# Quantised attention in a decoder kernel: constant waits, two heads scored together, the bias on GpSimd, four score slots

## The chip, the cores and the metric

One core of one Trainium2 chip. The metric is the device time of one execution in microseconds. The kernel is one program that holds a whole two-layer decoder; the change touches one of its stages.

## The reference, cut to what matters

Input x is 32 x 64 tokens of width 256, and ctx has the same shape. There are six sublayers; the fifth is the quantised cross-attention, with 16 heads of width 16 over all 2048 tokens at once (every query sees all 2048 keys):

```python
q = (x @ Wq + bq).reshape(1, B * N, H, hd)          # B*N = 2048, H = hd = 16
kv = (cond @ Wkv + bkv).reshape(1, -1, 2, H, hd)
q = _fq_sym(q * scale, axis=-1)                     # rounded to 127 steps per token and head
k = _fq_sym(k, axis=-1)
v = _fq_sym(v, axis=2)
attn = jax.nn.softmax(jnp.einsum('bhqd,bhkd->bhqk', q, k), axis=-1)
attn = _fq_unsigned(attn, axis=-1)                  # rounded to 255 steps of the row's maximum
out = jnp.einsum('bhqk,bhkd->bhqd', attn, v)
```

The row maximum of the softmax is always 255 steps, so exp(score - max + ln 255), rounded to an integer, is the quantised row up to its sum.

## The kernel before

The stage is `quantised_attention`. Its first block makes the quantised operands: `QT` (queries, transposed, bf16, 128 tile-and-head-pair slices; an even head's 48 rows begin at partition 0, an odd head's at 64), `KTt` (keys, likewise) and `Vi` (values as whole numbers). The second block is the loop that the change rewrites. It has 256 units: 16 tiles of 128 queries by 16 heads. A unit n is one head of one tile, 128 queries by 2048 keys. For each unit:

- TensorE (`score`) multiplies 48 rows by 512 keys four times, into two pairs of PSUM banks, a pair (1024 keys) for each half. Six of the eight banks serve as three such pairs, taken in turn (`pair_banks`). A group of two matmuls waits on `score_out` until the pair's earlier content was read, and raises `scored`.
- VectorE reads a pair with one `tensor_scalar` that also reduces: it scales by the negative query step `nsq`, writes 1024 fp32 scores to `S32` and their minimum to `mn`, and raises `score_out`. After both halves a 128x1 operation makes `ebias` = min of the two + ln 255 and raises `biased`. `S32` is the old context buffer `ctxT`, with two slots.
- ScalarE takes the exponential of the 2048 scores with that bias into `e16`, as uint16, with the sum in `esum`, and raises `exped`. There are four slots, in the buffers `xh` and `xl`.
- The sync engine issues a DMA transpose of `e16` to `PT` (four slots, in `xnT`), which lands on `laid[slot]`. It waits for `exped` and for the mix four units earlier.
- TensorE (`mix`), six units behind (`LAG`), multiplies 16 transposed blocks by `Vi` and raises `mixed`; after eight heads ScalarE copies the result out (`output`).
- GpSimd copies each pair's query slice from `QT` to one of six slots `Qs`, three pairs ahead, since a loop can't index `QT` for a weight load by a register as it is written here.

The order on each engine is written by hand. The first 48 units are written out, then a hardware loop (`Fori`) of four rounds has a body of 48 units whose waits and indices are worked out in registers, and the last 16 units and the drain are written out again. `wait_apart` is a wait followed by a separate semaphore instruction. Blocks end with all engines waiting for each other.

Of the kernel before, what the change touches and what calls it, by code (L numbers as in the profile page):

```python
# [23 lines left out]
ds = bass.ds  # L24
# [1334 lines left out]
def quantised_attention(nc, m, w):  # L1359
# [16 lines left out]
    q_here, scored, score_out, biased, exped, mixed, normed, chain2 = (m.sem(f"e_{n}") for n in (  # L1376
        "q_here", "scored", "score_out", "biased", "exped", "mixed", "normed", "chain2"))
# [4 lines left out]
    with ExitStack() as own:  # L1382
# [186 lines left out]


        class Unit:

            def __init__(self, i, u):
                self.i, self.u, self.j = i, u, u % H
                self.known = isinstance(i, int)

            def n(self, per=1, times=1):

                return self.i * (BODY // per * times) + self.u // per * times

            def back(self, d):
                return Unit(self.i, self.u - d)

            def exists(self):
                return not self.known or 0 <= self.i * BODY + self.u < N

            def at_least(self, k):

                return not self.known or self.i * BODY + self.u >= k

        def loop(eng, step, extra=0):

            for u in range(BODY):
                step(Unit(0, u))
            with eng.Fori(1, N // BODY) as i:
                for u in range(BODY):
                    step(Unit(i, u))
            for u in range(N % BODY + extra):
                step(Unit(N // BODY, u))
# [5 lines left out]
        with nc.Block() as block:  # L1605
            @block.gpsimd
            def _(pool):

                def fetch(x):

                    pair = x.n(2)
                    if x.at_least(2 * QSLOTS):
                        m.wait_apart(pool, scored, (pair - (QSLOTS - 1)) * 4)
                    pool.tensor_copy(Qs[:, x.u // 2 % QSLOTS, :],  # L1614
                                     QT[:, ds(pair, 1), :].rearrange("p a b -> p (a b)")).then_inc(q_here, 1)

                def step(x):
                    if not x.exists():
                        return
                    ahead = x.back(-2 * QAHEAD)  # L1620
                    if x.u % 2 == 0 and ahead.exists():
                        fetch(ahead)

                for p in range(QAHEAD):
                    fetch(Unit(0, 2 * p))
                loop(pool, step)

            @block.sync
            def _(sp):
                def step(x):  # L1630
                    m.wait_apart(sp, exped, x.n() + 1)
                    if x.at_least(SLOTS):
                        m.wait_apart(sp, mixed, x.n() - (SLOTS - 1))
                    sp.dma_start_transpose(PT[:, x.u % SLOTS, :, :], e16[x.u % SLOTS].bitcast(F16)).then_inc(laid[x.u % SLOTS], 16)
                loop(sp, step)

            @block.tensor
            def _(pe):
                def score(x):
                    j = x.j  # L1640
                    rows = slice(64 * (j % 2), 64 * (j % 2) + 48)
                    if j % 2 == 0:
                        m.wait_apart(pe, q_here, x.n(2) + 1)
                    for hf in range(2):
                        if x.at_least(2):
                            m.wait_apart(pe, score_out, x.n(1, 2) + hf - 2)
                        elif 2 * x.u + hf >= 3:
                            pe.wait_ge(score_out, 2 * x.u + hf - 2)
                        b = pair_banks(2 * x.u + hf)
                        for q in range(2):  # L1650
                            mm = pe.matmul(m.bank[b + q], Qs[rows, x.u // 2 % QSLOTS, :],  # L1651
                                           KTt[rows, j // 2, (2 * hf + q) * BLK:(2 * hf + q + 1) * BLK],
                                           start=True, stop=True)
                        mm.then_inc(scored, 1)

                def mix(x):
                    j = x.j
                    m.wait_apart(pe, laid[x.u % SLOTS], x.n(SLOTS, 16) + 16)
                    if j % 8 == 0 and x.at_least(16):
                        m.wait_apart(pe, normed, x.n(8) - 1)  # L1660
                    for k in range(KT):
                        mm = pe.matmul(m.bank[6 + j // 8][:, j % 8 * HD:(j % 8 + 1) * HD], PT[:, x.u % SLOTS, k, :],  # L1662
                                       Vi[:, k, j, :], start=(k == 0), stop=(k == KT - 1))
                    mm.then_inc(mixed, 1)

                def step(x):
                    if x.exists():
# [377 lines left out]
```

## Time and profile before

| | |
|---|---|
| three timed runs, median | 3037.68 us (3037.57 to 3043.3) |
| profiled execution | 3038.51 us |
| its span, first to last instruction | 3036.7 us |
| mean granted TensorE clock | 0.792 |
| TensorE matmuls busy | 2498.7 us, 82% |
| VectorE busy | 1932.5 us, 64% |
| ScalarE busy | 1482.0 us, 49% |
| GpSimd busy | 409.3 us, 13% |

Busy times are sums over the whole program, whose stages have different limits. A clock of 1.00 is 2.4 GHz and 0.50 is 1.2 GHz. PE is TensorE's matmuls, PEld its weight loads, DVE is VectorE, ACT is ScalarE, POOL is GpSimd, SPq the sync engine's queue. In brackets behind an instruction stand the idle time before it and what ended it.

### The profile page before, as it was taken

What the parts mean: (1) busy time and instruction counts of PE and PEld (TensorE: products, weight loads), DVE (VectorE), ACT (ScalarE), POOL (GpSimd) and SP (SyncE); (2) the same over time, 40 slices, a digit from 0 to 9 for tenths busy, and PEclk for the clock granted to TensorE, in tenths of its full rate; (3) what the DMA queues carried; (4) which work ended last, traced back from release to release, by engine and by line L of the source; (5) the groups of instructions that cost most, each with busy time, mean ns of one, the idle gap of its engine ahead of it and who ended that gap; (6) DMA issues with size and microseconds to landing.
All of it is one profiled execution on the core that took longest, in us unless ns stands there. A gap on an engine that the chain in (4) does not pass through costs nothing. (4 is left out here: it accounts for less than half of the span.)

```text
span 3036.7 us, 50228 instructions
## 1 busy us (share of the span) xinstructions
PE 2498.7 (82%) x16570; PEld 1358.9 (45%) x16570; DVE 1932.5 (64%) x3686; ACT 1482.0 (49%) x2055; POOL 409.3 (13%) x454
## 2 busy tenths in 40 slices
PE   6874775999979999999664888787878865999998
PEld 3333554555547777777552222222222232444444
DVE  6995556667743333333456998888888845666665
ACT  5552332444433333333232776666666633666664
POOL 0001220111012222333133000000000001001100
PEclk9886776999979999999776555555555567999999
DMA  2000000000010000000000999999999940000001
GB/s 83 0 0 19 0 0 12 16 26 21 21 29 18 18 17 17 17 17 9 21 0 18 177 176 169 165 169 162 171 163 171 173 71 17 24 23 16 23 23 36
DMA packets 594876, 175.35 MB, mean 58 GB/s; under 512 B 548642, under 2 KB 594212, under 8 KB 594724
## 3 DMA queue, kind: packets, MB, share of 16 engines
q1 hardware_dynamic: 594724, 173.44, 29.6%
q8 instruction: 81, 1.33, 0.2%
q14 instruction: 71, 0.58, 0.1%
HBM read 37.07 MB, written 2.10 MB: 13 GB/s over the span
## 5 line engine op out<-in xcount | busy, mean ns | idle before, releaser
L1682 DVE TENSOR_SCALAR_CACHE_REDUCE ctxT<-psum,e_nsq 128x1024 f32<-128x1024 f32 x512 | 637.2, 1282 | 74.2 <-issue 54.1
L1651 PE MATMUL psum<-e_KT,e_Qs 48*128 48x512 bf16 x1024 | 519.9, 611 | 181.7 <-DVE ctxT L1682 151.0
L1703 ACT ACTIVATE xh<-ctxT,e_ebias 128x2048 uint16<-128x2048 f32 x128 | 256.2, 2002 | 134.0 <-DVE e_ebias L1686 134.0
L1703 ACT ACTIVATE xl<-ctxT,e_ebias 128x2048 uint16<-128x2048 f32 x128 | 256.2, 2002 | 119.2 <-DVE e_ebias L1686 119.2
L1651 PEld LDWEIGHTS psum<-e_KT,e_Qs 48*128 48x128 bf16 x1024 | 67.3, 104 | 415.8 <-issue 408.1
L103 PE MATMUL psum<-xh,d_WT 128*128 128x512 f16 x768 | 229.4, 381 | 2.6 <-DVE d_WT L1214 2.6
L1662 PEld LDWEIGHTS psum<-e_Vi,xnT 128*128 128x128 f16 x4096 | 129.5, 105 | 216.8 <-issue 216.8
L1233 DVE TENSOR_TENSOR d_ACC<-psum,d_ACC 128x512 f32<-128x512 f32 x128 | 82.5, 686 | 171.1 <-PE psum L1287 171.1
L103 PE MATMUL psum<-xh,f_WA 128*128 128x512 f16 x544 | 152.7, 383 | 13.9 <-DVEq L1896 11.8
L103 PE MATMUL psum<-xh,c_Wx 128*128 128x512 f16 x576 | 161.3, 383 | 0.8 <-DVE X L960 0.8
L1662 PE MATMUL psum<-e_Vi,xnT 128*128 128x16 f16 x4096 | 152.5, 175 | 8.1 <-DMA xnT<-xh 4.5
L1912 DVE SCALAR_TENSOR_TENSOR X<-psum,f_route,X 128x256 f32<-128x256 f32 x272 | 112.8, 477 | 70.3 <-PE psum L1972 70.3
L1139 POOL TENSOR_TENSOR d_sq<-d_oS 128x512 f32<-128x512 f32 x64 | 99.1, 1548 | 420.8 <-ACT d_oS L1183 420.8
L1972 PE MATMUL psum<-f_W2H,f_hh 128*128 128x256 f16 x544 | 151.0, 278 | 3.1 <-DVE f_hh L1924 3.1
L1972 PE MATMUL psum<-f_W2L,f_hh 128*128 128x256 f16 (+1 forms) x544 | 150.8, 277 | 0.0
L1227 DVE SCALAR_TENSOR_TENSOR d_y<-d_gt,d_oS 128x512 f32<-128x512 f32 x64 | 44.3, 693 | 145.6 <-ACT d_oS L1183 145.6
L1614 POOL COPY e_Qs<-e_QT 128x128 bf16 (+1 forms) x128 | 37.3, 294 | 722.9 <-PE psum L1651 722.6
L1287 PE MATMUL psum<-d_WoT,d_y 128*128 128x256 f32 x512 | 122.7, 382 | 5.8 <-DVE d_y L1227 5.7
L974 DVE SCALAR_TENSOR_TENSOR X<-psum,c_route,X 128x256 f32<-128x256 f32 x288 | 119.3, 476 | 11.8 <-PE psum L103 11.0
L1875 ACT ACTIVATE f_h<-psum 128x512 f32<-128x512 f32 x68 | 40.6, 597 | 156.4 <-PE psum L103 156.4
L1902 DVE TENSOR_TENSOR f_pr<-psum,f_h 128x512 f32<-128x512 f32 x68 | 47.0, 692 | 108.9 <-ACT f_h L1875 108.9
L1167 ACT ACTIVATE d_kT<-psum 128x512 f32<-128x512 f32 x64 | 38.2, 597 | 159.3 <-PE psum L103 159.3
(312 smaller groups left out, 4965.9 us busy)
## 6 DMA issues: line engine op xcount, KB each, us to landing
d_Wn<-in_L_attn_w_qkv SPq DMA_DIRECT2D x16, 384.0 KB, 3.2
f_W<-in_L_ffn_w_routed SPq DMA_DIRECT2D x32, 176.0 KB, 2.5
ctx_rows<-in_ctx SPq DMA_DIRECT2D x1, 2048.0 KB, 8.6
X<-in_x SPq DMA_DIRECT2D x1, 2048.0 KB, 14.0
c_Wgu<-in_L_ffn_rg SPq DMA_DIRECT2D x16, 128.0 KB, 2.1
c_Wgu<-in_L_ffn_rw SPq DMA_DIRECT2D x16, 128.0 KB, 2.2
c_Wd<-in_L_ffn_rw SPq DMA_DIRECT2D x16, 128.0 KB, 2.2
d_Wn<-in_L_attn_w_gate SPq DMA_DIRECT2D x16, 128.0 KB, 3.0
```

The source lines that it names most:

```text
L103: mm = pe.matmul(out, lhsT(a, k), rhs(b, k), start=(n == 0), stop=(n == len(terms) - 1))
L974: last = dve.scalar_tensor_tensor(m.X[:, t, :], m.bank[4 + 2 * (q % 2) + j // 2][:, (j % 2) * D:(j % 2 + 1) * D], R.route[:, t, ds(e0 + sl ...
L1139: pool.tensor_tensor(sq[:, :], o, o, ALU.mult).then_inc(squared, 1)
L1233: last = dve.tensor_tensor(a2, m.bank[6 + half][:, :], a2, ALU.add)
L1287: mm = pe.matmul(m.bank[6 + j // 2][:, (j % 2) * D:(j % 2 + 1) * D], y[:, j * P:(j + 1) * P], WoT[:, slot, :], start=True, stop=True)
L1651: mm = pe.matmul(m.bank[b + q], Qs[rows, x.u // 2 % QSLOTS, :], KTt[rows, j // 2, (2 * hf + q) * BLK:(2 * hf + q + 1) * BLK], start=True, ...
L1662: mm = pe.matmul(m.bank[6 + j // 8][:, j % 8 * HD:(j % 8 + 1) * HD], PT[:, x.u % SLOTS, k, :], Vi[:, k, j, :], start=(k == 0), stop=(k == ...
L1682: dve.tensor_scalar(S32[:, sl, hf * HALF:(hf + 1) * HALF].rearrange("p (a b) -> p a b", a=2), m.psum[:, b:b + 2, :], nsq[:, ds(x.n(), 1)], ...
L1703: act.activation(e16[x.u % SLOTS], S32[:, x.u % 2, :], ACT.Exp, bias=ebias[:, x.u % 2:x.u % 2 + 1], scale=-1.0, accum_out=esum[:, ds(x.n() ...
L1902: dve.tensor_tensor(pr[:, st % 2, 0, :], m.bank[1][:, :], h1[:, st % 2, 0, :], ALU.mult).then_inc(product, 1)
L1912: last = dve.scalar_tensor_tensor(m.X[:, t, :], m.bank[4 + 2 * (q % 2) + j // 2][:, (j % 2) * D:(j % 2 + 1) * D], R.route[:, t, ds(e, 1)], ...
L1972: mm = pe.matmul(m.bank[4 + 2 * (q % 2) + j // 2][:, (j % 2) * D:(j % 2 + 1) * D], a, b, start=(n == 0), stop=(n == len(terms) - 1))
```

## The change

All of the loop is written out: `loop` calls a step for each of the 256 units with a plain number, so that waits and indices are constants, and `wait_apart` goes. TensorE reads its query weights from `QT` directly, and `Qs` with its copies and the semaphore `q_here` go. `score` is called for an even unit alone and scores it and the next one: in each half and quarter an even head's matmul (partitions 0 to 47) is followed by the odd head's (64 to 111), into two different bank pairs, four matmuls behind one wait. VectorE reads both heads' first halves, then both second halves. `ebias` is made by GpSimd, and `S32`, `mn` and `ebias` have four slots in place of two (`Smore` is new memory). The exponential, the transpose, the mix and the output keep their work.

```diff
-        BODY, SLOTS, LAG, QAHEAD, QSLOTS = 48, 4, 6, 3, 6
-        Qs = sb("Qs", [P, QSLOTS, P], BF16)
-        mn = sb("mn", [P, 2, 2])
-        ebias = sb("ebias", [P, 2])
+        SLOTS, LAG = 4, 6
+        mn = sb("mn", [P, SLOTS, 2])
+        ebias = sb("ebias", [P, SLOTS])
...
+        Smore = sb("Smore", [P, 2, TOK])
...
-        S32 = m.ctxT
+        S32 = [m.ctxT[:, 0, :], m.ctxT[:, 1, :], Smore[:, 0, :], Smore[:, 1, :]]
...
+        def loop(step, extra=0):
+
+            for n in range(N + extra):
+                step(n)
...
             @block.gpsimd
             def _(pool):
...
+                def step(n):
+                    sl = n % SLOTS
+                    pool.wait_ge(score_out, n // 2 * 4 + 3 + n % 2)
+                    if n >= SLOTS:
+                        pool.wait_ge(exped, n - SLOTS + 1)
+                    pool.tensor_scalar(ebias[:, sl:sl + 1], mn[:, sl, 0:1], mn[:, sl, 1:2], LN255,
+                                       ALU.min, ALU.add).then_inc(biased, 1)
...
             @block.sync
...
+                def step(n):
+                    sl = n % SLOTS
+                    sp.wait_ge(exped, n + 1)
+                    if n >= SLOTS:
+                        sp.wait_ge(mixed, n - SLOTS + 1)
+                    sp.dma_start_transpose(PT[:, sl, :, :], e16[sl].bitcast(F16)).then_inc(laid[sl], 16)
...
             @block.tensor
...
+                def score(n):
+
                     for hf in range(2):
...
+                        c = 2 * n + 2 * hf
+                        if c >= 2:
+                            pe.wait_ge(score_out, c - 1)
                         for q in range(2):
...
+                            col = (2 * hf + q) * BLK
+                            for odd in range(2):
+                                rows = slice(64 * odd, 64 * odd + 48)
+                                mm = pe.matmul(m.bank[pair_banks(c + odd) + q], QT[rows, n // 2, :],
+                                               KTt[rows, n % H // 2, col:col + BLK], start=True, stop=True)
                         mm.then_inc(scored, 1)
...
+                def step(n):
+                    if n % 2 == 0 and n < N:
+                        score(n)
+                    if n >= LAG:
+                        mix(n - LAG)
...
             @block.vector
...
+                def step(n):
+                    if n % 2:
+                        return
+                    if n >= SLOTS:
+                        dve.wait_ge(exped, n - SLOTS + 2)
                     for hf in range(2):
...
+                        dve.wait_ge(scored, n + hf + 1)
+                        for odd in range(2):
+                            sl = (n + odd) % SLOTS
+                            b = pair_banks(2 * n + 2 * hf + odd)
+                            dve.tensor_scalar(S32[sl][:, hf * HALF:(hf + 1) * HALF].rearrange("p (a b) -> p a b", a=2),
+                                              m.psum[:, b:b + 2, :], nsq[:, n + odd:n + odd + 1], None, ALU.mult, ALU.min,
+                                              accum_out=mn[:, sl, hf:hf + 1]).then_inc(score_out, 1)
...
             @block.scalar
...
+                    if n < N:
+                        act.wait_ge(biased, n + 1)
+                        if n >= SLOTS:
+                            act.wait_ge(laid[sl], 16 * (n // SLOTS))
+                        act.activation(e16[sl], S32[sl], ACT.Exp, bias=ebias[:, sl:sl + 1],
+                                       scale=-1.0, accum_out=esum[:, n:n + 1]).then_inc(exped, 1)
```

## Rows read from the trace of the kernel before

**Rows 1.** The page's 40 slices: busy tenths, TensorE's granted clock, DMA share.
```profile
DVE  6995556667743333333456998888888845666665
PEclk9886776999979999999776555555555567999999
DMA  2000000000010000000000999999999940000001
```

**Rows 2.** Groups of instructions, 1655 to 2456 us: VectorE's reductions.
```profile
L1682 DVE TENSOR_SCALAR_CACHE_REDUCE ctxT<-psum,e_nsq 128x1024 f32<-128x1024 f32 x512 | 637.2, 1282 | 74.2 <-issue 54.1 <-PE psum L1651 16.1
```

**Rows 3.** Timeline: VectorE's first and last operation of the stage.
```profile
1655.87 1.28 DVE L1682 TENSOR_SCALAR_CACHE_REDUCE ctxT<-psum,e_nsq 128x1024 f32<-128x1024 f32 x1 [10.62 <-PE psum L1651]
...
2451.95 0.21 DVE L1686 TENSOR_SCALAR e_ebias<-e_mn 128x1 f32<-128x1 f32 x1 [0.15 <-DVE ctxT L1682]
```

**Rows 4.** Timeline of a written-out unit: start, duration, engine, instruction, wait before it.
```profile
1715.23 1.28 DVE L1682 TENSOR_SCALAR_CACHE_REDUCE ctxT<-psum,e_nsq 128x1024 f32<-128x1024 f32 x1
...
1716.44 1.28 DVE L1682 TENSOR_SCALAR_CACHE_REDUCE ctxT<-psum,e_nsq 128x1024 f32<-128x1024 f32 x1
...
1717.61 0.51 PEld L1662 LDWEIGHTS psum<-e_Vi,xnT 128*128 128x128 f16 x16 [0.84 <-issue]
...
1717.88 0.21 DVE L1686 TENSOR_SCALAR e_ebias<-e_mn 128x1 f32<-128x1 f32 x1 [0.15 <-DVE ctxT L1682]
...
1718.16 1.28 DVE L1682 TENSOR_SCALAR_CACHE_REDUCE ctxT<-psum,e_nsq 128x1024 f32<-128x1024 f32 x1
1718.30 2.00 ACT L1703 ACTIVATE xh<-ctxT,e_ebias 128x2048 uint16<-128x2048 f32 x1 [0.84 <-DVE e_ebias L1686]
```

**Rows 5.** Timeline around a turn of the loop and of two looped units.
```profile
2100.10 1.86 PE L1651 MATMUL psum<-e_KT,e_Qs 48*128 48x512 bf16 x4 [3.62 <-DVE ctxT L1682]
...
2103.95 1.28 DVE L1682 TENSOR_SCALAR_CACHE_REDUCE ctxT<-psum,e_nsq 128x1024 f32<-128x1024 f32 x1 [4.50 <-PE psum L1651]
...
2107.05 1.28 DVE L1682 TENSOR_SCALAR_CACHE_REDUCE ctxT<-psum,e_nsq 128x1024 f32<-128x1024 f32 x1 [0.24 <-issue]
...
2110.15 1.28 DVE L1682 TENSOR_SCALAR_CACHE_REDUCE ctxT<-psum,e_nsq 128x1024 f32<-128x1024 f32 x1 [0.24 <-issue]
```

**Rows 6.** Groups of GpSimd, by form, whole run: its smallest operations.
```profile
L1614 POOL COPY e_Qs<-e_QT 128x128 bf16 x96 | 28.2, 294 | 578.3 <-PE psum L1651 578.3
...
L2033 POOL MEMSET const-float32-0.0<- 128x1 f32 x1 | 0.1, 98 | 0.2 <-issue 0.2
```

**Rows 7.** Timeline near the stage's start, where VectorE still waits for matmuls.
```profile
1659.89 1.28 DVE L1682 TENSOR_SCALAR_CACHE_REDUCE ctxT<-psum,e_nsq 128x1024 f32<-128x1024 f32 x1
...
1661.33 1.01 PE L1651 MATMUL psum<-e_KT,e_Qs 48*128 48x512 bf16 x2 [0.20 <-DVE ctxT L1682]
...
1662.13 1.99 ACT L1703 ACTIVATE xh<-ctxT,e_ebias 128x2048 uint16<-128x2048 f32 x1
...
1662.50 1.28 DVE L1682 TENSOR_SCALAR_CACHE_REDUCE ctxT<-psum,e_nsq 128x1024 f32<-128x1024 f32 x1 [0.96 <-PE psum L1651]
```

**Rows 8.** Timeline: small-tile matmuls of another stage; then a window with the clock.
```profile
409.36 1.11 PE L683 MATMUL psum<-b_Kbd,b_QT 64*64 64x256 f32 x16
...
409.30:410.50 1.20, 1.17 (x17) 0.57 (x16) 1.20 (x3) 0.27 (x1) 0.00 (x0) 1.00 0.00 0
```

**Rows 9.** Windows (last columns: clock, DMA share, GB/s), then timeline of the sync queue.
```profile
1664.00:1668.50 4.50, 3.39 (x8) 0.45 (x8) 4.06 (x9) 2.38 (x5) 0.29 (x1) 0.50 1.14 212
...
1696.50:1697.50 1.00, 1.00 (x16) 0.40 (x15) 0.85 (x3) 0.46 (x2) 0.00 (x0) 0.50 1.27 45
...
1694.88 2.99 SPq L1634 DMA_TRANSPOSE xnT<-xl  x1
...
2449.45 3.06 SPq L1634 DMA_TRANSPOSE xnT<-xh  x1
```

**Rows 10.** The transposes' line: time from issue to landing.
```profile
DMA to landing us min/median/max: 4.2/4.3/6.7
```

More of the change, by code:

```diff
@@ L1568, in quantised_attention @@
                for x in (m.xh, m.xl) for i in range(2)]
[L1571 to L1599, printed above, removed]
+        def loop(step, extra=0):
+            for n in range(N + extra):
+                step(n)
         def pair_banks(c):
@@ L1607, in _ @@
             def _(pool):
[L1609 to L1622, printed above, removed]
@@ L1637, in _ @@
+                loop(step)
             @block.tensor
             def _(pe):
[L1639 to L1643, printed above, removed]
-                    for hf in range(2):
[L1645 to L1649, printed above, removed]
-                        for q in range(2):
-                            mm = pe.matmul(m.bank[b + q], Qs[rows, x.u // 2 % QSLOTS, :],
-                                           KTt[rows, j // 2, (2 * hf + q) * BLK:(2 * hf + q + 1) * BLK],
-                                           start=True, stop=True)
-                        mm.then_inc(scored, 1)
@@ L1661, in mix @@
+                def mix(n):
+                    j = n % H
+                    pe.wait_ge(laid[n % SLOTS], 16 * (n // SLOTS + 1))
+                    if j % 8 == 0 and n >= 16:
+                        pe.wait_ge(normed, n // 8 - 1)
                     for k in range(KT):
-                        mm = pe.matmul(m.bank[6 + j // 8][:, j % 8 * HD:(j % 8 + 1) * HD], PT[:, x.u % SLOTS, k, :],
+                        mm = pe.matmul(m.bank[6 + j // 8][:, j % 8 * HD:(j % 8 + 1) * HD], PT[:, n % SLOTS, k, :],
@@ L1663, in mix @@
                                        Vi[:, k, j, :], start=(k == 0), stop=(k == KT - 1))
                     mm.then_inc(mixed, 1)
-                def step(x):
-                    if x.exists():
-                        score(x)
-                    if x.back(LAG).exists():
-                        mix(x.back(LAG))
-                loop(pe, step, LAG)
+                def step(n):
[3 more added lines that the diff above has]
+                        mix(n - LAG)
@@ L1673, in _ @@
+                loop(step, LAG)
             @block.vector
             def _(dve):
[L1675 to L1687 removed]
@@ L1690, in _, with output @@
+                loop(step)
             @block.scalar
             def _(act):
[L1692 to L1706 removed]
+                def output(n):
+                    t, half = n // H, n // 8 % 2
+                    act.wait_ge(mixed, n + 8)
+                    act.activation(Osb[:, t, half * P:(half + 1) * P], m.bank[6 + half][:, 0:P], ACT.Copy, scale=2.0 ** 24).then_inc(normed, 1)
@@ L1707, in step @@
                         output(done)
-                loop(act, step, LAG + 8)
+                loop(step, LAG + 8)
         rsum = sb("rsum", [P, N])
```

50 lines of the change are left out of this document (7 added, 43 removed).

## Prediction

> **What bounds the kernel now.** I read the slices first. The change lies in the attention loop, slices 23 to 33 or so, and there VectorE is busy 8 to 9 tenths, the DMA engines 9 tenths, and TensorE's granted clock is at 5 tenths, its lower level of 1.2 GHz [rows 1]. So there are two candidates: VectorE and the transposes. The groups of the stretch name VectorE's work: 512 reductions of 1282 ns [rows 2]. The first starts at 1655.87, the last small bias operation ends at 2452.16 [rows 3]. The stage is 796.3 us from one to the other, for 256 units (a unit is one head of one 128-query tile).
>
> The timeline of a written-out unit shows how VectorE spends it: half 0 starts at 1715.23, half 1 at 1716.44 (so 1.21 us for a reduction that isn't held up), the bias operation at 1717.88, the next unit at 1718.16 [rows 4]. A unit is 2.93 us: 2.42 us of reductions and 0.51 us for the bias operation with its waits on both sides. In the loop units start at 2107.05 and 2110.15, so 3.10 us, with 0.24 us in front of the first half that wait for nothing shown (register work), and at a turn of the loop VectorE stood 4.50 us for matmuls that came late [rows 5]. As a check: 48 + 16 written-out units by 2.93 are 187.5 us, 192 looped ones by 3.10 are 595.2, together 782.7; the 13.6 us left are 3.4 for each of four turns. VectorE bounds the stage, and everything else waits for it.
>
> **The change, part by part.**
>
> *Loop written out.* 192 units lose 0.17 us, 32.6 us, and the four turns go, 13.6 us. The first 48 units ran in this form, so the cost of straight code is in their 2.93 us.
>
> *Bias on GpSimd.* VectorE's floor becomes 2 x 1.21 = 2.42 us a unit. The hop is now VectorE, GpSimd, ScalarE. No 128x1 arithmetic of GpSimd is in the trace; the nearest rows are a 128x1 memset of about 0.10 us and a 128x128 copy of 0.29 us [rows 6]. I take 0.25 us, and 0.2 us for each handover (VectorE's bias operation ended at 1718.09, and ScalarE started at 1718.30 [rows 4]), so some 0.65 us from the last reduction to the exponential. It costs nothing as long as the four score slots cover it: the pair n needs the slots of pair n-4, whose two exponentials end 0.65 + 2 x 2.0 + 0.2 = 4.85 us after their third reduction (an exponential is 2.0 us [rows 4, 7]), while VectorE comes back to these slots 1.2 + 5.2 us after it at 2.6 us a unit. Slack 1.6 us, which would also cover a GpSimd operation of 1.8 us; what goes beyond it falls on VectorE once in every pair, half of it on each unit. ScalarE itself needs 2.0 to 2.2 us a unit and isn't the bound.
>
> *Q copies gone.* 128 copies of 0.29 us leave GpSimd, which idled; nothing on the path. The stage still starts behind the block before it, so I take nothing for the start.
>
> *Two heads at once.* Here a new chain arises. TensorE now fills two bank pairs (4 matmuls) behind one wait, score_out >= c-1, with three pairs in all. So chunks c and c+1 can't be begun before reduction c-2 has ended, and VectorE has only reduction c-1 (1.21 us) to work on meanwhile. The rows give each piece of this loop: reduction starts 1659.89, its release lets the matmuls start at 1661.33 (1.44 us), and the reduction that waits for them starts at 1662.50 (1.17 us) [rows 7]. That was for two matmuls in series on one row half, 1.01 us in all; four in series took 1.86 us at the loop's turn [rows 5], so each further one costs 0.43 us, which is its 512 columns at 1.2 GHz. If two heads on the two row halves really run at once, four take the time of two, and the loop is 1.44 + 1.17 = 2.61 us for two reductions, that is 2.61 us a unit against VectorE's floor of 2.42. VectorE should stand 0.2 us at each of 256 groups.
>
> Do they run at once? The trace has one place with small tiles: 16 fp32 matmuls of 256 columns on 64x64 tiles took 1.11 us in all at clock 1.00 [rows 8]. One after the other, at a column a cycle of 2.4 GHz, they would take 1.71 us at the least: tiles overlap there. In that place row and column halves both change, so it doesn't prove it for rows alone.
>
> The Trainium skill, page "TensorE: Matmul & The Clock Gate", Part 3, says that matmuls on different row groups run concurrently, a pack costing one matmul plus about 4 ns for each further tile. By that the sum would be 1 us higher (256 x 0.004) than by my rows. It agrees with rows 8 in direction; no run here shows it for rows alone yet.
>
> The two mixes behind a pair (0.51 us of weight loads each [rows 4]) start when the second group is issued and end about 1.1 us later, before the next release 1.44 us after VectorE's third start. They stay hidden.
>
> *The transposes* are what is late next. Each moves 0.524 MB. While two of them ran back to back the engines moved 212 GB/s, so 2.47 us each; now and then the stream drops, as to 45 GB/s for 1.0 us [rows 9]. The sync queue's 2.99 us transpose at 1694.88 is the same event; between it and the last, at 2449.45, I count 64 above 2.5 us, and one before them, in 256; the rest are near 1.9 [rows 9]. A drop loses about 1.0 x (212-45)/212 = 0.8 us, a quarter of the units have one, so 0 to 0.2 us a unit (nothing, if the stream catches up), and the transposes need 2.47 to 2.67 us a unit, if a drop costs only what the engines lose. At 2.93 this was hidden; at 2.61 it is not quite. Landing takes 4.3 us from issue, 6.7 at most [rows 10]; a slot is needed again four units later, 10.4 us, from which 2.2 us of exponential and about 1 us of waiting for the mix go off, so one drop is absorbed, a run of them isn't.
>
> I take 2.64 us a unit: 2.61 of the chain and 0.03 for drops that come too close together. The pairing delays the first exponential by a reduction or so: 1.5 us once. Sum, against the profiled execution (3038.5 us, its span 3036.7; the median of the three timed runs is 3037.7, 0.8 lower): 3038.5 - 796.3 + 1.5 + 256 x 2.64 = 3038.5 - 794.8 + 675.8 = 2919.5, and 2919 for the median.
>
> The Trainium skill's page "DMA: Bandwidth & Descriptors", Latency and other measured facts, gives a DMA transpose an effective 261 GB/s. By that a transpose here would take 2.01 us and could never bind; the sum would stay at the chain, 2912. The rows show 212 GB/s in both transposes that ran back to back, so the measurement decides, and the transposes stay within 0.2 us of the chain.
>
> **Rivals.**
> - *The transposes bind.* Backlogged, each drop costs in full. The longest sync-queue entries are 1.1 us above the usual, in 65 of 256: 2.47 + 0.28 = 2.75 us a unit, 2948; with gaps between transposes 2.80, 2961. For it: a DMA share of 9 tenths already at 2.93. Against: half a microsecond of each unit was idle between them.
> - *TensorE's clock rises or the waits are shorter than read.* At 2.4 GHz the group takes some 0.6 instead of 1.0 us, the chain falls to 2.2 and VectorE's 2.42 is left; the transposes then allow 2.47 to 2.58: 2876 to 2904. For it: twice the rows work at once. Against: the clock stood at 0.50 with TensorE busy most of the time.
> - *No overlap of the row halves: slower.* Then four matmuls in series hold VectorE: 2.61 + 2 x 0.43 = 3.47 us a unit, 3132. It decides from the point where a group takes 0.49 us more than two matmuls do (3.10 us a unit is the stage of now). Against it: rows 8. This is also the case in which the pairing doesn't do what it says.
> - *Two engines trade waits* (late landing holds the exponential, that holds the slots, that the scores): 2.8 to 3.1 us a unit, 2960 to 3037. Slack of 1.6 us and more at each handover speaks against it.
>
> **How the numbers follow.** Chain at 2.58 to 2.70 us a unit, 2904 to 2935: 55%. Transposes bind, 2935 to 2961: 17%. Clock or shorter waits, 2876 to 2904: 13%. Traded waits: 5% faster, 2% level. No overlap: 8% slower. The first three are the range, 2876 to 2961, 85%. Within 0.2% (6 us, about what a measurement of this kernel can tell from no change) there is almost only the last bit of the traded waits: 2%. Faster 90%, slower 8%.
>
> **What the changed profile would show.** VectorE's reductions 1.21 us apart in twos, then about 0.2 us idle put down to the score matmuls, some 50 us in all; four score matmuls in about 1.0 us; units 2.6 us apart throughout; no turn gaps; no VectorE bias work; ScalarE waiting for GpSimd's bias and hardly for landings. The DMA rate near 200 GB/s. If waits of TensorE's mixes or of ScalarE for the transposes add up to more than 20 us, the transposes bind. If four score matmuls take 1.9 us, the pairing failed. If the clock reads 1.00 in the stage, the chain went away. Wrong altogether would be a stage whose units are 3.1 us or more apart.

## The result and the profile after

| | before | after |
|---|---|---|
| median, us | 3038.53 (3037.57 to 3043.3, 4 runs) | 2922.46 (2922.12 to 2923.73, 4 runs) |
| span of the profiled execution, us | 3036.7 | 2920.3 |
| VectorE, first to last operation of the stage, us | 796.3 [rows 3] | 673.5 |
| a unit, us | 2.93 written out, 3.10 looped | 2.63 |

The ratio is 0.9616, with an interval of 0.9599 to 0.9632: 3.8% faster. The prediction was 2919, with 2.64 us a unit.

The stage gives 122.8 us and its start comes 0.8 us earlier. The tail takes some back: from VectorE's last operation to the reciprocal behind the stage it is 14.2 us now and was 9.3 before, and what follows that takes 577.4 us instead of 575.2. So -122.8 - 0.8 + 4.9 + 2.2 = -116.5, against 3036.7 - 2920.3 = 116.4.

The page's slices of after, for VectorE, TensorE's granted clock, the DMA share and the DMA rate. They answer to [rows 1].

```profile
DVE  6995647577763333333355799999999845666665
PEclk9896776899979999999977655555555567999999
DMA  2000000000010000000000299999999910000001
GB/s 87 0 0 19 1 0 12 11 22 27 22 26 19 19 18 18 15 12 18 10 22 0 44 197 198 199 200 199 199 201 198 201 31 9 16 24 24 16 24 37
```

The DMA row has nine full slices, each of 73.0 us, where it had ten of 75.9; the clock in it is still 0.50 of full speed (1.2 GHz), and VectorE looks fuller than before. The last row is the one to stop at: 197 to 201 GB/s in every slice of the stage, with no slice lower. One transpose of 0.524 MB at 199 GB/s is 2.63 us, which is the unit. An even rate alone proves no limit: with the loop written out and nothing else (an experiment below), VectorE sets the pace, and the slices read 178 to 181 GB/s. What tells more is whether the sync queue stands between its entries, which the transposes' rows below show.

The groups of the stage in after (busy us, mean ns | idle us before them and what ended it; the first two answer to [rows 2]):

```profile
L1647 DVE TENSOR_SCALAR_CACHE_REDUCE ctxT<-psum,e_nsq 128x1024 f32<-128x1024 f32 x256 | 314.7, 1282 | 29.1 <-ACT xh L1665 17.9 <-PE psum L1614 10.1
L1647 DVE TENSOR_SCALAR_CACHE_REDUCE e_Smore<-psum,e_nsq 128x1024 f32<-128x1024 f32 x256 | 314.7, 1282 | 24.2 <-ACT xl L1665 23.1
...
L1665 ACT ACTIVATE xl<-e_Smore,e_ebias 128x2048 uint16<-128x2048 f32 x128 | 255.9, 1999 | 72.4 <-DMA xnT<-xl 67.9 <-POOL e_ebias L1588 3.7
L1665 ACT ACTIVATE xh<-ctxT,e_ebias 128x2048 uint16<-128x2048 f32 x128 | 255.9, 1999 | 70.9 <-DMA xnT<-xh 62.0 <-POOL e_ebias L1588 8.5
...
L1624 PE MATMUL psum<-e_Vi,xnT 128*128 128x16 f16 x4096 | 140.9, 175 | 36.2 <-DMA xnT<-xl 21.1 <-DMA xnT<-xh 14.8
...
L1588 POOL TENSOR_SCALAR e_ebias<-e_mn 128x1 f32<-128x1 f32 x256 | 73.3, 286 | 602.0 <-DVE e_Smore L1647 292.8 <-DVE ctxT L1647 288.5 <-ACT xl L1665 10.8
```

Two things promised in the prediction are missing. VectorE stands only 10.1 us on the score matmuls, all of it once at the stage's start, not 50. And ScalarE stands 67.9 + 62.0 = 129.9 us on landings of transposes, the mixes another 35.9. VectorE's 41.0 us on exponentials are the same wait passed on: landing, exponential, score slot, reduction.

The timeline of after (start, duration; the idle time before in brackets), at the stage's start, in its course and at its end:

```profile
1655.11 1.28 DVE L1647 TENSOR_SCALAR_CACHE_REDUCE ctxT<-psum,e_nsq 128x1024 f32<-128x1024 f32 x1 [10.09 <-PE psum L1614]
...
1658.94 0.32 POOL L1588 TENSOR_SCALAR e_ebias<-e_mn 128x1 f32<-128x1 f32 x1 [5.26 <-DVE ctxT L1647]
1659.30 2.00 ACT L1665 ACTIVATE xh<-ctxT,e_ebias 128x2048 uint16<-128x2048 f32 x1 [4.02 <-POOL e_ebias L1588]
...
1709.54 1.28 DVE L1647 TENSOR_SCALAR_CACHE_REDUCE e_Smore<-psum,e_nsq 128x1024 f32<-128x1024 f32 x1
...
1710.75 1.28 DVE L1647 TENSOR_SCALAR_CACHE_REDUCE e_Smore<-psum,e_nsq 128x1024 f32<-128x1024 f32 x1
1710.89 1.04 PE L1614 MATMUL psum<-e_KT,e_QT 48*128 48x512 bf16 x4 [1.59 <-DVE e_Smore L1647]
...
1711.92 2.00 ACT L1665 ACTIVATE xh<-ctxT,e_ebias 128x2048 uint16<-128x2048 f32 x1 [0.39 <-DMA xnT<-xh]
...
1711.97 1.28 DVE L1647 TENSOR_SCALAR_CACHE_REDUCE e_Smore<-psum,e_nsq 128x1024 f32<-128x1024 f32 x1
...
2328.57 0.08 DVE L1647 DVE_READ_ACCUMULATOR e_Smore<-psum,e_nsq 128x1 f32 x1
2342.86 1.75 DVE L1680 RECIPROCAL e_rsum<-e_esum 128x256 f32<-128x256 f32 x1 [14.20 <-PEq L1579]
```

The chain that I had put at 2.61 us is in the middle rows. The reduction starts at 1709.54 and the four matmuls at 1710.89 (1.35 us, predicted 1.44). The reduction behind them starts at 1711.97 (1.08 us, predicted 1.17). That is 2.43 us for two reductions, and VectorE's own 2 x 1.21 lets it start no earlier: the chain is 2.43 us at most in this place. (From one pair of heads to the next it is a little longer, as the first experiment shows.) Meanwhile ScalarE, at 1711.92, waits for a transpose to land.

The transposes' line in after: issues on the sync queue (duration min/median/max in ns), then issue to landing. It answers to [rows 9, 10].

```profile
L1599 SPq DMA_TRANSPOSE xnT<-xh x128: 1642/2512/3915, 1661.4 to 2332.1; - x128
L1599 SPq DMA_TRANSPOSE xnT<-xl x128: 1791/2409/3680, 1666.8 to 2337.1; - x128
DMA to landing us min/median/max: 4.3/4.8/6.8
```

Before, most entries were near 1.9 us, because the queue was empty when a transpose came. Now the median is 2.4 to 2.5 us: each is issued into a full queue. Landing went from 4.3 to 4.8 us. Entries of 2.9 us and more, the drops of the stream, number 56.

The timeline of the sync queue, before and after, each row two entries:

```profile
1703.66 4.71 SPq L1634 DMA_TRANSPOSE xnT<-xl  x2
1709.52 5.70 SPq L1634 DMA_TRANSPOSE xnT<-xh  x2
...
1704.91 4.62 SPq L1599 DMA_TRANSPOSE xnT<-xh  x2
1709.62 4.71 SPq L1599 DMA_TRANSPOSE xnT<-xl  x2
```

Before, the first row ends at 1708.37 and the next entry starts 1.15 us later; in after it is 0.09 us. Over the stage the median gap between entries was 1.10 us and is 0.09, and in after only 7 of 255 gaps are above 0.2 us. The transposes follow each other without a break, and ScalarE and the mixes wait for them.

VectorE's units in after aren't evenly 2.63 us apart, as a mean would suggest: half of them are 2.43 us or less apart, and the waits of 41.0 us fall between pairs of heads.

### The profile page after: what moved, and what is told of

The parts are those of the page before. It is cut to its first block and busy times, and to the rows that moved or that the text cites. A ratio compares the mean times of both kernels' runs of the same rounds, so it can differ in the third digit from the quotient of the medians.

```text
span 2920.3 us, 45877 instructions
## 1 busy us (share of the span) xinstructions
PE 2256.0 (77%) x16570; PEld 1321.5 (45%) x16570; DVE 1868.6 (64%) x3430; ACT 1476.6 (51%) x2055; POOL 445.2 (15%) x582
## 5 line engine op out<-in xcount | busy, mean ns | idle before, releaser
L1614 PE MATMUL psum<-e_KT,e_QT 48*128 48x512 bf16 x1024 | 265.1, 618 | 279.3 <-DVE e_Smore L1647 130.3
L1647 DVE TENSOR_SCALAR_CACHE_REDUCE ctxT<-psum,e_nsq 128x1024 f32<-128x1024 f32 x256 | 314.7, 1282 | 29.1 <-ACT xh L1665 17.9
L1647 DVE TENSOR_SCALAR_CACHE_REDUCE e_Smore<-psum,e_nsq 128x1024 f32<-128x1024 f32 x256 | 314.7, 1282 | 24.2 <-ACT xl L1665 23.1
L1665 ACT ACTIVATE xl<-e_Smore,e_ebias 128x2048 uint16<-128x2048 f32 x128 | 255.9, 1999 | 72.4 <-DMA xnT<-xl 67.9
L1614 PEld LDWEIGHTS psum<-e_KT,e_QT 48*128 48x128 bf16 x1024 | 33.8, 107 | 406.9 <-DVE e_Smore L1647 193.6
L1624 PE MATMUL psum<-e_Vi,xnT 128*128 128x16 f16 x4096 | 140.9, 175 | 36.2 <-DMA xnT<-xl 21.1
L1588 POOL TENSOR_SCALAR e_ebias<-e_mn 128x1 f32<-128x1 f32 x256 | 73.3, 286 | 602.0 <-DVE e_Smore L1647 292.8
L103 PE MATMUL psum<-xh,f_WA 128*128 128x512 f16 x544 | 152.7, 383 | 13.9 <-DVEq L1858 11.8
```

The source lines that it names most:

```text
L103: mm = pe.matmul(out, lhsT(a, k), rhs(b, k), start=(n == 0), stop=(n == len(terms) - 1))
L1588: pool.tensor_scalar(ebias[:, sl:sl + 1], mn[:, sl, 0:1], mn[:, sl, 1:2], LN255, ALU.min, ALU.add).then_inc(biased, 1)
L1614: mm = pe.matmul(m.bank[pair_banks(c + odd) + q], QT[rows, n // 2, :], KTt[rows, n % H // 2, col:col + BLK], start=True, stop=True)
L1647: dve.tensor_scalar(S32[sl][:, hf * HALF:(hf + 1) * HALF].rearrange("p (a b) -> p a b", a=2), m.psum[:, b:b + 2, :], nsq[:, n + odd:n + od ...
L1665: act.activation(e16[sl], S32[sl], ACT.Exp, bias=ebias[:, sl:sl + 1], scale=-1.0, accum_out=esum[:, n:n + 1]).then_inc(exped, 1)
```

## The experiments

Each run but the last is one execution; beside them before took 3037.5 to 3038.1 us. A difference of some 6 us between two of them is no difference.

### Half the bytes in each transpose

```diff
-sp.dma_start_transpose(PT[:, sl, :, :], e16[sl].bitcast(F16)).then_inc(laid[sl], 16)
+sp.dma_start_transpose(PT[:, sl, 0:KT // 2, :], e16[sl][:, 0:TOK // 2].bitcast(F16)).then_inc(laid[sl], 16)
...
-PT[:, n % SLOTS, k, :]
+PT[:, n % SLOTS, k % (KT // 2), :]
```

> The changed kernel with only the first half of each unit transposed (1024 of 2048 scores; the mix multiplies the blocks of that half twice, so its matmuls and their number stay, and the output isn't the attention any more). The changed kernel takes 2.63 us a unit (673.5 us of VectorE for 256). If the transposes bind it, units fall to VectorE's own 2.42 or the chain's 2.43 us, and the time falls by 256 x 0.20 = 51 us, from 2922 to about 2871. If the chain through VectorE and TensorE binds at 2.61 us, as I forecast, nothing falls: 2922, and VectorE still stands 0.2 us in each group.

Measured: 2874.8 us, where 2871 was expected. The groups' first row of the stage, a window in its middle (us; busy us and count of PE, PEld, DVE, ACT, POOL; clock, DMA share, GB/s), and a timeline across the border between two pairs of heads:

```profile
L1647 DVE TENSOR_SCALAR_CACHE_REDUCE ctxT<-psum,e_nsq 128x1024 f32<-128x1024 f32 x256 | 314.7, 1281 | 3.0 <-PE psum L1614 1.6
```

```profile
1900.00:2100.00 200.00, 122.71 (x1632) 48.57 (x1629) 199.12 (x323) 166.07 (x173) 23.19 (x81) 0.50 0.58 107
```

```profile
1901.04 1.28 DVE L1647 TENSOR_SCALAR_CACHE_REDUCE e_Smore<-psum,e_nsq 128x1024 f32<-128x1024 f32 x1
1901.18 1.04 PE L1614 MATMUL psum<-e_KT,e_QT 48*128 48x512 bf16 x4 [0.44 <-DVE e_Smore L1647]
...
1902.34 1.28 DVE L1647 TENSOR_SCALAR_CACHE_REDUCE ctxT<-psum,e_nsq 128x1024 f32<-128x1024 f32 x1
...
1903.55 1.28 DVE L1647 TENSOR_SCALAR_CACHE_REDUCE ctxT<-psum,e_nsq 128x1024 f32<-128x1024 f32 x1
...
1904.77 1.28 DVE L1647 TENSOR_SCALAR_CACHE_REDUCE ctxT<-psum,e_nsq 128x1024 f32<-128x1024 f32 x1
```

With 107 GB/s VectorE is busy 199.12 of 200 us, and ScalarE waits for no landing any more. So the transposes set after's time. VectorE's stage, first to last operation, falls from 673.5 to 633.4 us, 2.47 us a unit, and the tail by another 6.4 us (14.2 to 7.8).

The 2.47 isn't quite VectorE's own 2.42. Within a pair of heads the reductions start 1.21 or 1.22 us apart, but over the border to the next pair it is 1.30 us (1901.04 to 1902.34), with matmuls that end at 1902.22, just before. The gap is too short for the view of waits, and no run tells whether the matmuls or the additional wait for the exponentials make it. So the chain, or something beside it, holds VectorE by 0.05 us a unit at most, not by 0.2.

### Pairing undone, bias on GpSimd and four slots kept

```diff
-c = 2 * n + 2 * hf
-if c >= 2:
-    pe.wait_ge(score_out, c - 1)
+c = 2 * n + hf
+if c >= 3:
+    pe.wait_ge(score_out, c - 2)
+rows = slice(64 * (n % 2), 64 * (n % 2) + 48)
```

> The changed kernel with the pairing undone: one head at a time, two matmuls of one row half behind each wait, a bank pair each; loop written out, bias on GpSimd and four slots stay. If the transposes bind, the pairing is worth nothing and the time stays at 2922 (within 6 us). If the forecast chain bound, taking it away frees VectorE down to 2.42 to 2.5 us a unit: 2870 to 2890. If TensorE needs the pairing (1.7 us of scores and 0.5 us of mix in series), units grow beyond 2.7 us: over 2940.

Measured: 2926.15 us, 4 us above after, at 197 to 198 GB/s. VectorE waits 64 us for scores here, and the timeline of TensorE shows where much of that comes from: the mix stands 1.76 us for a landing, and the scores come behind it in the program's order. So this too is the transposes' wait passed on. The pairing's effect on its own engine is real: four matmuls in series on one half take 1.88 us, and in after 1.04 us.

```profile
1903.89 0.59 PE L1623 MATMUL psum<-e_Vi,xnT 128*128 128x16 f16 x16 [1.76 <-DMA xnT<-xh]
...
1904.42 1.88 PE L1613 MATMUL psum<-e_KT,e_QT 48*128 48x512 bf16 x4
```

### Bias back on VectorE, the rest as in after

```diff
+for odd in range(2):
+    sl = (n + odd) % SLOTS
+    dve.wait_ge(score_out, 2 * n + 3 + odd)
+    dve.tensor_scalar(ebias[:, sl:sl + 1], mn[:, sl, 0:1], mn[:, sl, 1:2], LN255,
+                      ALU.min, ALU.add).then_inc(biased, 1)
```

> The changed kernel with the two bias operations of a pair back on VectorE, behind its four reductions. By the rows of before (0.21 us an operation, 0.15 us of wait before it, 0.07 us after) that is about 0.72 us in a pair, so VectorE needs 2.42 + 0.36 = 2.78 us a unit. Transposes bind now: the unit goes from 2.63 to 2.78 and the time to about 2961. Were the moved bias worth its whole 0.5 us a unit, it would be 3000 or more; were it hidden, 2922.

Measured: 2929.07 us. The expectation of 2961 took 0.36 us a unit for the bias from rows of before, and it fell. The timeline of VectorE, the first reduction of a pair, its bias operations and the next pair:

```profile
1919.36 1.27 DVE L1642 TENSOR_SCALAR_CACHE_REDUCE ctxT<-psum,e_nsq 128x1024 f32<-128x1024 f32 x1
...
1924.19 0.33 DVE L1648 TENSOR_SCALAR e_ebias<-e_mn 128x1 f32<-128x1 f32 x2
1924.44 1.27 DVE L1642 TENSOR_SCALAR_CACHE_REDUCE e_Smore<-psum,e_nsq 128x1024 f32<-128x1024 f32 x1
```

Both bias operations of a pair take 0.33 us together, and the pair takes 5.08 us where nothing is waited for (1919.36 to 1924.44): VectorE needs 2.54 us a unit and is still under the transposes' 2.63. The run is 6.6 us above after, but VectorE's stage only 2.8 us longer; the rest lies outside it.

### Order of the four score matmuls

```diff
-for q in range(2):
-    col = (2 * hf + q) * BLK
-    for odd in range(2):
+for odd in range(2):
+    for q in range(2):
+        col = (2 * hf + q) * BLK
```

> The changed kernel with the four matmuls of a group ordered even, even, odd, odd instead of even, odd, even, odd. Same work and waits. If matmuls overlap only with a neighbour on the other row half, three waves of 0.43 us take the place of two and the group's chain goes from 2.43 to 2.86 us a unit: 2922 + 256 x 0.23 = 2981. If the halves don't depend on the order, nothing changes: 2922. If this order overlaps nothing, 3.29 us a unit: 3091.

Measured: 2923.32 us. The four still take 1.04 us (timeline of TensorE), though the two of one row half now stand next to each other:

```profile
1901.17 1.04 PE L1614 MATMUL psum<-e_KT,e_QT 48*128 48x512 bf16 x4 [1.49 <-DVE e_Smore L1647]
```

### The kernel before with its loop written out, and nothing else

```diff
-            for u in range(BODY):
+            for u in range(N + extra):
                 step(Unit(0, u))
-            with eng.Fori(1, N // BODY) as i:
-                ...
```

> The kernel before with nothing but its loop written out (Q copies, separate semaphore instructions, bias on VectorE, two slots, one head at a time stay). VectorE binds in both theories: 256 units of 2.93 us instead of 192 of 3.10 and four turns, so 3038 - 32.6 - 13.6 = 2992. If straight code costs more than the first 48 units showed (instruction loads that hold an engine), it is above 3000.

Measured: 2998.07 us, 40 us less than before, where the prediction had 32.6 + 13.6 = 46. VectorE's timeline has units 2.93 us apart, as the first 48 units had in before:

```profile
1901.09 1.28 DVE L1677 TENSOR_SCALAR_CACHE_REDUCE ctxT<-psum,e_nsq 128x1024 f32<-128x1024 f32 x1
...
1902.53 0.21 DVE L1681 TENSOR_SCALAR e_ebias<-e_mn 128x1 f32<-128x1 f32 x1
1902.81 1.28 DVE L1677 TENSOR_SCALAR_CACHE_REDUCE ctxT<-psum,e_nsq 128x1024 f32<-128x1024 f32 x1
```

### The same, and plain waits in place of the separate ones

`wait_apart` is a wait followed by a semaphore instruction of its own (`eng.wait_ge(sem, value)`, then `eng.sem_inc(self.apart, 1)`). The change took them all out of this loop. On top of the last kernel this one does that alone. The bias on VectorE, one head at a time, the Q copies and the two score slots stay.

```diff
-m.wait_apart(dve, scored, x.n(1, 2) + hf + 1)
+dve.wait_ge(scored, x.n(1, 2) + hf + 1)
...
-m.wait_apart(dve, score_out, x.n(1, 2) + 2)
+dve.wait_ge(score_out, x.n(1, 2) + 2)
```

(and eleven more of the kind on the five engines)

> The kernel before with its loop written out and, in addition, the 13 kinds of waits of this loop without the separate semaphore instruction behind them. Bias on VectorE, two slots, Q copies and one head at a time stay. The run that only wrote the loop out took 2998 (2.93 us a unit). The half-transpose pair showed that the separate instructions behind two kinds of waits cost 0.2 us a unit. If they are what made VectorE's bias cost 0.51 us a unit, VectorE needs 2.42 + 0.21 + 0.05 to 0.15 = 2.7 to 2.8 us a unit: 2940 to 2965. If the bias operation with its dependence costs that by itself, 2998 stays.

Measured: 2923.23 us, below the 2940 to 2965 expected, and all but 1 us of the change's gain without its other parts. VectorE's timeline of a unit:

```profile
1900.66 1.27 DVE L1677 TENSOR_SCALAR_CACHE_REDUCE ctxT<-psum,e_nsq 128x1024 f32<-128x1024 f32 x1
...
1901.86 1.28 DVE L1677 TENSOR_SCALAR_CACHE_REDUCE ctxT<-psum,e_nsq 128x1024 f32<-128x1024 f32 x1
...
1903.18 0.21 DVE L1681 TENSOR_SCALAR e_ebias<-e_mn 128x1 f32<-128x1 f32 x1
1903.31 1.27 DVE L1677 TENSOR_SCALAR_CACHE_REDUCE ctxT<-psum,e_nsq 128x1024 f32<-128x1024 f32 x1
```

The bias operation itself is 0.21 us in both kernels. From the second reduction's start to it there were 1.44 us and are 1.32, from it to the next unit 0.28 and now 0.13: together 0.27 of the 0.28 us that a unit lost (2.93 to 2.65). The first of these steps has one separate instruction in it, the second has two (behind the waits for the exponentials and for the scores). A fourth, between the unit's two reductions, costs next to nothing: they start 1.20 us apart here and 1.21 us with it. 256 x 0.28 = 72 us, of the 75 measured. None of these instructions has a row in the views of busy time; only the distances between rows show them.

A window of this kernel has the DMA rate at 198 GB/s already, so VectorE (2.65) and the transposes (2.63) are nearly level here. VectorE still comes last, as ScalarE waits only 2.2 us for landings in the whole stage:

```profile
1900.00:2100.00 200.00, 190.31 (x1518) 57.78 (x1518) 197.28 (x379) 158.91 (x162) 11.25 (x38) 0.50 1.16 198
```

### After without the pairing and without the move to GpSimd

```diff
-pool.tensor_scalar(ebias[:, sl:sl + 1], mn[:, sl, 0:1], mn[:, sl, 1:2], LN255,
-                   ALU.min, ALU.add).then_inc(biased, 1)
...
-c = 2 * n + 2 * hf
+c = 2 * n + hf
...
+dve.wait_ge(score_out, 2 * n + 2)
+dve.tensor_scalar(ebias[:, sl:sl + 1], mn[:, sl, 0:1], mn[:, sl, 1:2], LN255,
+                  ALU.min, ALU.add).then_inc(biased, 1)
```

> The changed kernel with both the pairing and the move to GpSimd undone; written out, plain waits, queries read in place and four slots stay. If both are worth next to nothing because the transposes bind at 2.63 us a unit (undone one by one they cost 4 and 7 us), it stays within 2925 to 2945; VectorE by itself would need 2.7 to 2.8 us, which makes 2940 to 2965 if it becomes the bound again. If the two parts matter together, it goes back towards 2998.

Measured: 2925.97 us, at 197 to 199 GB/s. It is the kernel above approached from the other side, and it agrees: VectorE's stage is 679.6 us in both. The two differ in the Q copies and in two or four score slots, so these two parts together are worth nothing that can be seen at this speed.

### Half transposes, and separate waits again at two places

```diff
-pe.wait_ge(score_out, c - 1)
+m.wait_apart(pe, score_out, c - 1)
...
-dve.wait_ge(scored, n + hf + 1)
+m.wait_apart(dve, scored, n + hf + 1)
```

> As the run with half of each transpose (same work left out), and in addition the waits of the score matmuls and of the reductions are again followed by a separate semaphore instruction, as in the kernel before. With the transposes out of the way this shows the chain alone. If these extra instructions are what made my rows of before read 2.61 us (1.44 + 1.17) instead of the 2.43 us (1.35 + 1.08) that the changed kernel shows, units go from 2.43 to about 2.6 us, some 2915 to 2920 in all. If not, it equals the other half-transpose run.

Measured: 2917.01 us, against 2874.8 for the first experiment, of which it is an edit: 42 us for two instructions a unit, 0.16 us a unit. The timeline of VectorE and TensorE:

```profile
1900.09 1.28 DVE L1647 TENSOR_SCALAR_CACHE_REDUCE ctxT<-psum,e_nsq 128x1024 f32<-128x1024 f32 x1
...
1901.53 1.03 PE L1614 MATMUL psum<-e_KT,e_QT 48*128 48x512 bf16 x4 [1.60 <-DVE ctxT L1647]
...
1902.74 1.28 DVE L1647 TENSOR_SCALAR_CACHE_REDUCE ctxT<-psum,e_nsq 128x1024 f32<-128x1024 f32 x1 [0.15 <-PE psum L1614]
```

1.44 + 1.21 = 2.65 us: this is the chain of the prediction, with its very first piece, 1.44. It existed in the kernel before because these two instructions were in it.

### Every other block in the mix

```diff
-for k in range(KT):
+for k in range(0, KT, 2):
```

> The changed kernel with the mix multiplying every other block only (8 matmuls and 8 weight loads a unit instead of 16; the output isn't the attention any more). TensorE isn't the bound, so this alone gives nothing. It takes 4096 of TensorE's instructions out of the stage. If the drops in the transpose stream come from loading instructions, the long entries on the sync queue (59 of 2.9 us and more in the changed kernel) fall by a third and the DMA rate rises from 199 to some 205 GB/s, 2.56 us a unit: 2904. If the drops have another cause, 2922 and as many long entries.

Measured: 2910.91 us. It was to tell whether the drops of the transposes come with the loading of instructions, since it takes away 2048 matmuls and as many weight loads. The packets of the page's queue "q8 instruction" go from 71 to 55 (first row). Below it stands what such a packet looks like in after: in the 2 us from 1684 the same queue has one, and for a microsecond the engines move 4 GB/s:

```profile
q8 instruction: 55, 0.90, 0.1%
...
q8 instruction: 1, 0.02, 3.0%
...
1685.00:1686.00 1.00, 0.00 (x0) 0.00 (x0) 1.00 (x3) 0.98 (x2) 0.06 (x1) 0.50 0.04 4
```

Entries of 2.9 us and more go from 56 to 39, by the third that was expected. A window of 200 us has 203 GB/s, against 198 to 200 in after, and the time falls by 11.5 us of the 18 expected.

The edit also frees TensorE and its reads of SBUF, so by itself it doesn't prove instruction loading. The traces add that the two come together. In after, 53 of the 56 long entries have a packet of an instruction queue in them or up to 0.5 us ahead, and 8 of the other 200. In this run it is 37 of 39 and 9 of 217; before, with 2.5 us as the border, 64 of 65 and 7 of 191. So the drops go with the loading of instructions. That the packet is what stops the stream is the likely reading, but no run sends one without the other.

### Fifteen of sixteen blocks transposed

```diff
+sp.dma_start_transpose(PT[:, sl, 0:KT - 1, :], e16[sl][:, 0:TOK - P].bitcast(F16)).then_inc(laid[sl], 16)
...
+PT[:, n % SLOTS, min(k, KT - 2), :]
```

> The changed kernel with 15 of 16 blocks of each unit transposed (1920 of 2048 scores; the mix multiplies the 15th block twice, so TensorE's work stays, and the output isn't the attention). If the transposes bind in proportion to what they move, a unit takes 15/16 of 2.63 = 2.47 us, and the time falls by 41 us to 2881. If a fixed part of each transpose binds (issue, landing), it stays near 2922.

Measured: 2887.59 us. Fifteen sixteenths of 2.63 are 2.47, so 256 x 0.16 = 41 us were to be had if only bytes counted, and 35 came, as VectorE's 2.47 us lie in the way. VectorE's idle time is down to some 8 us, with 199 GB/s still moving: transposes and VectorE are nearly level at this size.

### One transpose for two units

```diff
+if n % 2:
+    return
...
+both = (m.xh, m.xl)[sl // 2][:, :, :].rearrange("p a b -> p (a b)")
+sp.dma_start_transpose(PT[:, sl:sl + 2, :, :].rearrange("p s k q -> p (s k) q"), both).then_inc(laid[sl], 16)
```

> The changed kernel with one transpose for two units (1 MB, into two neighbouring slots) instead of one each. If the sync queue's fixed work for each transpose sets the 2.63 us, the rate rises and the time falls below 2910. If it is the amount moved, the longer way from exponential to landing (two exponentials of 2.0 us, then about 7 us to land, with only two pairs of slots and 10.5 us for the round) makes units longer, 2.8 us or so: 2960 or more.

Measured: 2995.49 us. The window of its middle:

```profile
1900.00:2100.00 200.00, 104.00 (x1378) 41.07 (x1375) 168.46 (x275) 140.39 (x147) 19.47 (x68) 0.50 0.98 180
```

The rate is 180 GB/s. A double transpose waits for both exponentials and frees its slots only when all of it has landed, so the queue runs empty between them, and ScalarE waits 221 us for landings. What it leaves open is whether a double one is cheaper by itself: on the queue each takes 4.8 to 5.4 us, no better than two of 2.4 to 2.5.

### The sixteenth block turned by TensorE

All that bound after were bytes of transposes, with TensorE busy 6 tenths and ScalarE 8. So one of the sixteen blocks goes another way: TensorE transposes it for both heads of a pair into a PSUM bank, and one ScalarE copy of 256 columns puts it where the mix reads it.

```diff
-sp.dma_start_transpose(PT[:, sl, :, :], e16[sl].bitcast(F16)).then_inc(laid[sl], 16)
+sp.dma_start_transpose(PT[:, sl, 0:KT - 1, :], e16[sl][:, 0:TOK - P].bitcast(F16)).then_inc(laid[sl], 16)
...
+for odd in range(2):
+    mm = pe.transpose(m.bank[7].bitcast(F16)[:, odd * P:(odd + 1) * P],
+                      e16[(p + odd) % SLOTS].bitcast(F16)[:, TOK - P:], ident16[:, :])
+mm.then_inc(flipped, 1)
...
+act.activation(PTu[:, sl:sl + 2, KT - 1, :],
+               m.bank[7].bitcast(U16)[:, 0:2 * P].rearrange("p (s q) -> p s q", s=2),
+               ACT.Copy).then_inc(flip_out, 1)
```

(the mixes of all 16 heads then share bank 6, and the output is copied once per 16 heads)

> A version that should beat both kernels: the changed kernel with the last of a unit's 16 blocks turned by TensorE into a PSUM bank of its own (both heads of a pair, then one copy of 256 columns by ScalarE), and 15 blocks by DMA. All mixes share the other bank, and the output is copied once for 16 heads. Nothing is left out. The run with 15 blocks transposed and the 16th left out took 2888. If the transposes are all that binds, this comes to 2885 to 2895, as ScalarE has the room (2.03 us a unit, and some 0.2 more for the copies, of 2.5) and TensorE too. If the new handovers (exponential, TensorE, ScalarE, mix) come last instead, units stay at 2.6 us or more: 2915 and up.

Measured: 2889.47 us (2887.04 to 2889.8, 4 runs), ratio to before 0.9508, interval 0.9493 to 0.9524. That is 33.0 us below after, 1.1%, and the two intervals of the ratio (0.9493 to 0.9524 and 0.9599 to 0.9632) lie apart. Groups and a window of its stage:

```profile
L1669 DVE TENSOR_SCALAR_CACHE_REDUCE ctxT<-psum,e_nsq 128x1024 f32<-128x1024 f32 x256 | 314.6, 1281 | 7.4 <-ACT xh L1696 3.5 <-PE psum L1629 2.3 <-issue 0.4
...
L1685 ACT ACTIVATE xnT<-psum 128x256 uint16<-128x256 uint16 x128 | 46.5, 363 | 0.6 <-PE psum L1615 0.6
```

```profile
1900.00:2100.00 200.00, 134.97 (x1673) 53.31 (x1674) 196.60 (x321) 176.38 (x206) 23.01 (x80) 0.50 1.17 198
```

VectorE, the transposes and ScalarE (176.38 of 200 us) are all near full. A second block would take another 0.18 us of ScalarE a unit, for at most the 11.8 us that VectorE still idles.

## Why the prediction was right, and where it wasn't

The number was right and the mechanism wasn't, so a good part of the hit is luck. The prediction took 2.64 us a unit from a chain of 2.61 us and 0.03 us for drops. That chain is 2.43 us, and what takes 2.63 us is the transposes. They were a rival, with 2.75 us and 2935 to 2961 us (17%); the measured 2922 lies in the range given to the chain (2904 to 2935, 55%).

- **The loop written out.** Predicted -46 us, measured -40. Right in the main.
- **Bias on GpSimd.** The handovers are quicker than the 0.2 us taken: the read of the accumulator ended at 1658.83, GpSimd started at 1658.94, and 0.04 us after its end ScalarE starts. Its operation is 0.29 us (estimate 0.25). But what leaves VectorE was mis-sized: "0.51 us for the bias operation with its waits on both sides" is 0.23 us of bias (2.65 less 2.42 in the run with plain waits) and 0.28 us of separate semaphore instructions.
- **The removal of `wait_apart` was priced at nothing.** This is the step that failed. The diff shows it at every wait of the loop, and no sentence of the prediction costs it. It is worth 75 us, two thirds of the gain (measured on top of the loop written out). The sum still came out, because its cost was inside the 0.51 us and so went to the wrong edit.
- **Two heads at once, the chain.** The term 1.44 + 1.17 = 2.61 us is 1.35 + 1.08 = 2.43 us. Both pieces were read in [rows 7] from code in which a separate semaphore instruction stood behind the wait, and each carried 0.09 us or more of it. Put back, they gave 2.65. So the same error sits in two terms: too much off VectorE by the bias, too much on it by the chain. The trace of before holds the plain price too. There the first matmul group that waits for a reduction has a plain wait, and it starts 1.35 us after the first reduction's start at 1655.87 [rows 3]:

```profile
1657.22 1.03 PE L1651 MATMUL psum<-e_KT,e_Qs 48*128 48x512 bf16 x2 [0.68 <-DVE ctxT L1682]
```

- **The row halves overlap.** Right: four matmuls in 1.04 us, against 1.88 us in series. The Trainium skill's page "TensorE: Matmul & The Clock Gate", Part 3, has a pack of row groups at one matmul and about 4 ns for each further tile. The trace agrees in direction and nearly in size: four matmuls on two halves took 1.04 us, where two of one half took 1.01 us [rows 7].
- **The transposes.** The sum of the terms was right: 2.47 us and 0 to 0.2 us for drops gave "2.47 to 2.67 us a unit", and it is 2.63. What was wrong is to rank them below the chain, and to give them 2.75 us where they bind. The test that the prediction named (more than 20 us of waits for transposes) answers 165.8 us: 129.9 of ScalarE and 35.9 of the mixes.
- **The rate.** The stream was hardly ever idle for want of work in after and stood at 197 to 201 GB/s. The Trainium skill's page "DMA: Bandwidth & Descriptors" (Latency and other measured facts) gives a DMA transpose 261 GB/s with a non-contiguous middle dimension, and more for a contiguous one. This case doesn't reach that, so the measurement decides.
- **The clock** stayed at 0.50. Right.
- **Start and tail.** 1.5 us were added for a first exponential that comes later. It didn't: it starts 4.19 us after the first reduction in after and 4.26 us before. 4.9 us more came at the tail, which I had not costed: with the transposes late, the last of them are issued at 2332.1 and 2337.1, after VectorE's last operation.

Step by step, as the runs have it: 3038 before; 2998 written out; 2923 with plain waits; 2922 with pairing, GpSimd's bias, direct Q and four slots. The last four parts take what VectorE needs from 2.65 to 2.47 us a unit, and almost none of it shows, since the transposes need 2.63: the stage is 6.1 us shorter than with plain waits alone (673.5 instead of 679.6), and the tail, 14.2 us instead of 9.8, takes 4.4 of them back. It is there, though: with half the bytes VectorE runs at 2.47, and the last experiment collects 33 us of it.

What stays open: whether the instruction packets cause the drops that they come with, and what sets the rate of the transposes between drops (some 212 GB/s as a rule, but 287 GB/s in the microsecond from 1687 to 1688, behind the drop shown above). The Q copies and the score slots weren't tried each by itself. Nor was the pairing undone with the transposes out of the way, so no run shows that it helps there; two heads scored one by one might leave VectorE nearer to its 2.42 us.

## What to carry to other kernels

Price every instruction that an edit removes, also those that occupy no engine: a semaphore instruction between a wait and the work behind it lies on the path of each handover at which the engine stands and waits. A chain put together from rows of the old code carries that code's overheads; ask of each row what stood in its gap. And when three limits lie within 0.2 us of each other (here 2.47, 2.63 and 2.65), the sum can't rank them: halve the load of one and see whether the time moves.

## What was not expected of the hardware

- A separate semaphore instruction behind a wait costs 0.09 to 0.13 us at each handover between engines (1.44 against 1.35 us, 1.21 against 1.08). On VectorE one of them between a reduction and the bias operation that needs its result costs 0.12 us, two in front of the next unit 0.15 us, and one between two reductions of 1.21 us only 0.01. In this loop that was 75 us of 2998.
- Matmuls on the two row halves overlap whichever order they are issued in: even, odd, even, odd and even, even, odd, odd both took 1.04 us.
- DMA transposes of 128x2048 two-byte elements held 197 to 201 GB/s over 670 us in every slice of 73 us, though single ones took 1.6 to 3.9 us on the queue, and single microseconds had from 4 to 295 GB/s.
- Nearly every long transpose has a packet of an instruction queue beside it (53 of 56 in after, where it is 8 of the other 200).
